# Gated attention and ternary feed-forward block: another order of the step on all engines, quantiser halves and evictions on ScalarE, scale factors on GpSimd

## What is computed

```python
x = x + tanh(g_xattn) * mlstm(layernorm(x), ctx, ctx)   # 8 heads of 64
x = x + tanh(g_ffn)   * ffn(layernorm(x))
# mlstm, a head: log_D[i,j] = cs[i] - cs[j] + ig[j], j <= i;  D = exp(log_D - rowmax)
#   C = (q @ k.T / 8) * D;  h = C / max(|sum C|, exp(-rowmax)) @ v;  then RMS norm of h
# ffn: g, u = actq(x) @ ternary(w_gate).T, actq(x) @ ternary(w_up).T
#   h = relu(g)**2 * u;  out = actq(h) @ ternary(w_down).T
# actq: round(x * 127 / rowmax|x|), rescaled afterwards
```

## Time and profile before

| | |
|---|---|
| median of three runs | 704.64 us |
| profiled execution, its own time | 707.75 us |
| span of the profile | 706.0 us |
| TensorE matmul busy | 602.2 us, 85% |
| VectorE busy | 568.5 us, 81% |
| ScalarE busy | 424.0 us, 60% |
| GpSimd busy | 97.9 us, 14% |
| mean granted TensorE clock | 0.944 of full |

### The profile page before, as it was taken

The page is one execution under the profiler, slowest core; times in us unless marked ns, Lnnn a source line. Parts: engine busy times, 40 slices in busy tenths (PEclk is TensorE's granted clock), DMA queues, the critical chain, the costliest instruction groups (busy, mean ns, idle before and its releaser), DMA issues.

```text
span 706.0 us, 18248 instructions
## 1 busy us (share of the span) xinstructions
PE 602.2 (85%) x6596; PEld 347.4 (49%) x6596; DVE 568.5 (81%) x1288; ACT 424.0 (60%) x893; POOL 97.9 (14%) x170
## 2 busy tenths in 40 slices
PE   7384776989989898998989898989989898989887
PEld 4151433545545454554646454555546464556443
DVE  4388559797879879697988979797979889797965
ACT  4376894657466465757556565657466565666542
POOL 1165020101001010101001010101000010101000
PEclk9797888999999999999999999999999999999999
DMA  9945201304040220404040230405040311402000
GB/s 311 381 160 177 85 0 56 127 17 165 3 165 15 97 82 15 164 0 164 15 164 15 64 116 15 164 0 179 0 164 15 108 72 38 144 17 76 2 30 31
DMA packets 45168, 63.73 MB, mean 90 GB/s; under 512 B 1872, under 2 KB 26704, under 8 KB 45136
## 3 DMA queue, kind: packets, MB, share of 16 engines
q1 hardware_dynamic: 43024, 61.19, 24.8%
q10 hardware_dynamic: 2112, 2.11, 0.9%
HBM read 54.77 MB, written 8.52 MB: 90 GB/s over the span
## 4 chain that ended last, share of the span: by engine, by line
DVE 31%; PE 29%; issue 20%; ACT 12%; DMA 5%; DVEq 1%; POOL 1%; SPq 0%; ACTq 0%; POOLq 0%
PE gb L1032 9%; PE ub L1032 7%; ACT dmat L528 4%; DVE stage L721 4%; PE yb L1055 4%; DVE dmat L824 3%; DVE hmaxes L729 3%; PE ab L1063 3%; DMA dmat<-max_rows 3%; ACT dmat L522 2%; PE tp L1076 2%; DVE ssq L842 2%; DVE amax L883 2%; PE ab L1043 2%; DVE x L865 1%
## 5 line engine op out<-in xcount | busy, mean ns | idle before, releaser
L1032 PE MATMUL gb<-wgT,xqT 128*128 128x512 bf16 x512 | 145.3, 410 | 4.9 <-ACT xqT L509 2.8
L1032 PE MATMUL ub<-wuT,xqT 128*128 128x512 bf16 x512 | 141.9, 403 | 0.9 <-DVE stage L721 0.9
L1055 PE MATMUL yb<-wdT,stage 128*128 128x512 bf16 x512 | 120.6, 379 | 2.0 <-ACT stage L502 1.9
L488 ACT ACTIVATE relu<-gb 128x512 f32<-128x512 f32 x128 | 75.6, 590 | 50.7 <-PE gb L1032 49.7
L721 DVE TENSOR_TENSOR stage<-relu,ub 128x512 f32<-128x512 f32 x128 | 86.7, 681 | 14.3 <-ACT relu L490 13.6
L424 POOL TENSOR_SCALAR_AFFINE_SELECT dmat<-dmat 128x256 f32<-128x256 f32 x128 | 50.1, 416 | 303.4 <-ACT dmat L528 303.4
L824 DVE SCALAR_TENSOR_TENSOR dmat<-ab,dmat 128x384 f32<-128x384 f32 x128 | 65.3, 551 | 26.3 <-POOL dmat L424 19.5
L1032 PEld LDWEIGHTS ub<-wuT,xqT 128*128 128x128 bf16 x512 | 52.4, 104 | 67.6 <-issue 17.2
L1063 PE MATMUL ab<-qT,cT 64*128 64x256 f32 x256 | 59.0, 436 | 29.5 <-DVE dmat L824 29.5
L490 ACT ACTIVATE relu<-relu 128x512 f32<-128x512 f32 x128 | 80.7, 630 | 4.0
L1055 PEld LDWEIGHTS yb<-wdT,stage 128*128 128x128 bf16 x512 | 48.7, 98 | 58.1 <-ACT stage L502 1.8
(11 more groups left out here) (108 smaller groups left out, 802.0 us busy)
## 6 DMA issues: line engine op xcount, KB each, us to landing
dmat<-max_rows SPq DMA_DIRECT2D x14, 1024.0 KB, 5.1
values<-in_ctx_v SPq DMA_DIRECT2D x16, 520.0 KB, 7.5
xs<-in_x SPq DMA_DIRECT2D x16, 512.0 KB, 5.8
cT<-in_ctx_t SPq DMA_DIRECT2D x16, 512.0 KB, 6.8
out<-stage SPq DMA_DIRECT2D x32, 256.0 KB, 2.1
stage<-in_w_gate SPq DMA_DIRECT2D x4, 1024.0 KB, 13.5
stage<-in_w_up SPq DMA_DIRECT2D x4, 1024.0 KB, 17.4
stage<-in_w_down SPq DMA_DIRECT2D x4, 1024.0 KB, 5.6
```

Of the source, the lines that this page charges most:

```text
L488: nc.scalar.activation(relu[:, c % 2, :], gb[c % 2][:, :], ACT.Relu).then_inc(g_free, 1)
L1032: last = nc.tensor.matmul(bank[c % 2][:, :], xqT[par][:, t, d, :], w[:, d, c * CH:(c + 1) * CH], start=(d == 0), stop=(d == KD - 1))
L1055: done = nc.tensor.matmul(yb[:, :], hqT[:, c, :], wdT[:, c, :], start=(c == 0), stop=(c == KF - 1))
```

## The change

It does five things.

1. The order of `step` on TensorE, ScalarE and VectorE is new. Scores, `weigh` and head outputs of n open the step, with the four chunks of the first tile between them. The front of m and the end of attention of n stand in the middle. The first pairs of heads of m are exponentiated and masked at the step's end, the other two pairs of n at its start. Second chunks, maxima and quantisation of the second tile come last.
2. The upper half of a hidden tile is quantised by ScalarE (`quantise_high`), the lower by VectorE (`quantise_low`). `hq` has two buffers.
3. Both halves of the transposed hidden tile leave PSUM through ScalarE.
4. `dd`, `dd2`, `c3` (`token_factor`) and `dq` (`hidden_factor`) are made by GpSimd; VectorE waits on `c3_ready` and `dq_ready`.
5. The maximum over a hidden row is folded by writing the first three chunks' maximum behind the row and reducing from there, in place of a separate maximum of two.

The diff, cut to its core, the indentation reduced. Of the four long `step` functions, all but GpSimd's and SyncE's are shown in their new order alone (lines added and kept); their old order is in the kernel above.

```diff
-GATE_K, POST_K, LN2_K = 3, 11, 16
-QUANT_K = 9
+GATE_K, POST_K, LN2_K = 3, 11, 13
+QUANT_K = 6
...
+HW = FF + 512
+h = [stage[1][:, HW * t:HW * t + FF + 1] for t in range(T)]
...
-hq = sb("hq", [P, FF], F16)
+hq = [sb(f"hq{t}", [P, FF], F16) for t in range(T)]
...
 def step(b, n, m, par):
+    if m is not None:
+        spread_max(m, par)
     if not at(b, 0):
         store(b - 1, 1)
-    store(b, 0)
-    if m is not None:
-        spread_max(m, par)
     if m is not None and not at(m, LAST):
         load(m + 1, 1 - par)
+    store(b, 0)
...
+def token_factor(n, npar):
+    gp.wait_ge(ln2_step, LN2_K * n + 10)
+    alone(gp, gp_passed)
+    nc.gpsimd.tensor_scalar(dd[:, :], am2[:, :], 1.0 / 127.0, 0.0, ALU.mult, ALU.add).then_inc(token_scale, 1)
+    gp.wait_ge(token_scale, 3 * n + 1)
+    nc.gpsimd.tensor_tensor(dd2[:, :], dd[:, :], dd[:, :], ALU.mult).then_inc(token_scale, 1)
+    gp.wait_ge(token_scale, 3 * n + 2)
+    if at(n, 0):
+        gp.wait_ge(winv_step, WINV[1] + 2)
+    alone(gp, gp_passed)
+    nc.gpsimd.tensor_scalar(dd2[:, :], dd2[:, :], wprod[:, 1:2], 0.0, ALU.mult, ALU.add).then_inc(token_scale, 1)
+    gp.wait_ge(token_scale, 3 * n + 3)
+    nc.gpsimd.tensor_tensor(c3[npar][:, :], dd2[:, :], dd[:, :], ALU.mult).then_inc(c3_ready, 1)
+def hidden_factor(b, t):
+    gp.wait_ge(quant_step, QUANT_K * (2 * b + t) + 3)
+    if at(b, 0) and t == 0:
+        gp.wait_ge(winv_step, WINV[2] + 1)
+    alone(gp, gp_passed)
+    nc.gpsimd.tensor_scalar(dq[:, t:t + 1], hm1[:, t:t + 1], wprod[:, 2:3], 0.0, ALU.mult, ALU.add).then_inc(dq_ready, 1)
...
+token_factor(0, 0)
+masks(1, 0)
+masks(1, 1)
 def step(b, n, m, par):
-    if n is None:
-        return
-    for p in range(NP):
-        masks(n, p)
+    if n is not None:
+        masks(n, 2)
+        masks(n, 3)
     if at(b, 0):
         scale_weight(2, 0)
         scale_weight(2, 1)
-    residual(n, 1 - par)
+    hidden_factor(b, 0)
+    if n is not None:
+        residual(n, 1 - par)
+        token_factor(n, 1 - par)
+    hidden_factor(b, 1)
+    if m is not None:
+        masks(m, 0)
+        masks(m, 1)
...
 def hidden_cols(b, t):
-    act.wait_ge(a_full[0], hidden_use(b, t) + 1)
     if not (at(b, 0) and t == 0):
         act.wait_ge(y_full, 2 * b + t)
-    nc.scalar.activation(hqT[:, 0:KF // 2, :], abh[0].rearrange("p (k s) -> p k s", s=P), ACT.Copy,
-                         bias=-MAGIC16).then_inc(a_free[0], 1)
+    for e in range(2):
+        act.wait_ge(a_full[e], hidden_use(b, t) + 1)
+        nc.scalar.activation(hqT[:, e * KF // 2:(e + 1) * KF // 2, :], abh[e].rearrange("p (k s) -> p k s", s=P), ACT.Copy,
+                             bias=-MAGIC16).then_inc(a_free[e], 1)
+def quantise_high(b, t):
+    act.wait_ge(quant_step, QUANT_K * (2 * b + t) + 5)
+    nc.scalar.activation(hq[t][:, FF // 2:], h[t][:, FF // 2:FF], ACT.Copy, scale=hqs[:, t:t + 1],
+                         bias=MAGIC16).then_inc(hq_high, 1)
...
+exponentials(1, 0, 1)
+exponentials(1, 1, 1)
 def step(b, n, m, par):
     npar = 1 - par
     prev = not at(b, 0)
     third = at(b, 0)
+    if n is not None:
+        exponentials(n, 2, npar)
+        exponentials(n, 3, npar)
     relu_square(b, 0, 0)
+    if n is not None:
+        heads(n, 0)
     if third:
         magnitudes(2, 0, 4)
+    relu_square(b, 0, 1)
+    if m is not None:
+        attention_rstd(m)
+    if n is not None:
+        heads(n, 1)
+    if third:
+        magnitudes(2, 1, 5)
+    relu_square(b, 0, 2)
+    if n is not None:
+        heads(n, 2)
+        heads(n, 3)
+    if m is not None:
+        for t in range(T):
+            columns(m, qT[par], t)
+    relu_square(b, 0, 3)
+    if n is not None:
+        squares(n)
     if prev:
         hidden_cols(b - 1, 1)
     if third:
         magnitudes(2, 2, 6)
         magnitudes(2, 3, 7)
+    if m is not None:
+        forget_gate(m)
+    if n is not None:
+        head_rms(n)
+    quantise_high(b, 0)
     relu_square(b, 1, 0)
     if third:
         scale_weight(2, 2)
         scale_weight(2, 3)
         sign_weight(2, 0, 4)
+    relu_square(b, 1, 1)
+    if n is not None:
+        tokens_rstd(n)
+    hidden_cols(b, 0)
+    if third:
         sign_weight(2, 1, 4)
+    relu_square(b, 1, 2)
+    if n is not None:
+        quantise_second(n)
+    if m is not None:
+        exp_minus_max(m, par)
     if third:
         sign_weight(2, 2, 4)
         sign_weight(2, 3, 4)
     relu_square(b, 1, 3)
+    if m is not None:
+        exponentials(m, 0, par)
+    quantise_high(b, 1)
     if n is not None:
         tokens(n, npar)
+    if m is not None:
+        exponentials(m, 1, par)
...
 def hidden_max(b, t, part):
-    split = (3, 2)[t]
-    first, last = ((0, split), (split, NC))[part]
-    dve.wait_ge(h_done, 8 * b + 4 * t + last)
-    nc.vector.tensor_reduce(hmaxes[:, t, part:part + 1], h[t][:, first * CH:last * CH], axis=AX_X, op=ALU.max,
-                            apply_absolute_value=True).then_inc(quant_step, 1)
-
-def quantise_hidden(b, t, par):
-    hidden_max(b, t, 1)
+    if part == 0:
+        dve.wait_ge(h_done, 8 * b + 4 * t + 3)
+        nc.vector.tensor_reduce(h[t][:, FF:FF + 1], h[t][:, 0:3 * CH], axis=AX_X, op=ALU.max,
+                                apply_absolute_value=True).then_inc(quant_step, 1)
+    else:
+        dve.wait_ge(h_done, 8 * b + 4 * t + 4)
+        dve.wait_ge(quant_step, QUANT_K * (2 * b + t) + 1)
+        nc.vector.tensor_reduce(hmax[:, t:t + 1], h[t][:, 3 * CH:FF + 1], axis=AX_X, op=ALU.max,
+                                apply_absolute_value=True).then_inc(quant_step, 1)
+def hidden_scale(b, t, par):
     k = QUANT_K * (2 * b + t) + 2
+    if t == 0:
+        dve.wait_ge(c3_ready, b + 1)
     dve.wait_ge(quant_step, k)
-    nc.vector.tensor_tensor(hmax[:, t:t + 1], hmaxes[:, t, 0:1], hmaxes[:, t, 1:2], ALU.max).then_inc(quant_step, 1)
-    dve.wait_ge(quant_step, k + 1)
+    if not (at(b, 0) and t == 0):
+        dve.wait_ge(dq_ready, 2 * b + t)
     nc.vector.tensor_scalar(hm1[:, t:t + 1], hmax[:, t:t + 1], c3[par][:, t:t + 1], QUANT_EPS,
                             ALU.mult, ALU.max).then_inc(quant_step, 1)
+    dve.wait_ge(quant_step, k + 1)
+    nc.vector.reciprocal(rhm[:, t:t + 1], hm1[:, t:t + 1]).then_inc(quant_step, 1)
     dve.wait_ge(quant_step, k + 2)
-    nc.vector.reciprocal(rhm[:, t:t + 1], hm1[:, t:t + 1]).then_inc(quant_step, 1)
-    dve.wait_ge(quant_step, k + 3)
     nc.vector.tensor_scalar(hqs[:, t:t + 1], rhm[:, t:t + 1], c3[par][:, t:t + 1], 127.0,
                             ALU.mult, ALU.mult).then_inc(quant_step, 1)
-    dve.wait_ge(quant_step, k + 4)
-    if at(b, 0) and t == 0:
-        dve.wait_ge(winv_step, WINV[2] + 1)
-    for e in range(2):
-        half = slice(e * FF // 2, (e + 1) * FF // 2)
-        nc.vector.tensor_scalar(hq[:, half], h[t][:, half], hqs[:, t:t + 1], MAGIC16, ALU.mult, ALU.add).then_inc(quant_step, 1)
-    nc.vector.tensor_scalar(dq[:, t:t + 1], hm1[:, t:t + 1], wprod[:, 2:3], None, ALU.mult).then_inc(quant_step, 1)
-
-def hidden_cols(b, t):
-
-    dve.wait_ge(a_full[1], hidden_use(b, t) + 1)
-    if not (at(b, 0) and t == 0):
-        dve.wait_ge(y_full, 2 * b + t)
-    nc.vector.tensor_scalar(hqT[:, KF // 2:KF, :], abh[1].rearrange("p (k s) -> p k s", s=P), MAGIC16, None,
-                            ALU.subtract).then_inc(a_free[1], 1)
+def quantise_low(b, t):
+    dve.wait_ge(quant_step, QUANT_K * (2 * b + t) + 5)
+    nc.vector.tensor_scalar(hq[t][:, 0:FF // 2], h[t][:, 0:FF // 2], hqs[:, t:t + 1], MAGIC16,
+                            ALU.mult, ALU.add).then_inc(quant_step, 1)
 def output(b, t, xpar):
     k = 2 * b + t
     dve.wait_ge(y_full, k + 1)
-    dve.wait_ge(quant_step, QUANT_K * (k + 1))
+    dve.wait_ge(dq_ready, k + 1)
...
-        dve.wait_ge(o_ready, 2 * n - 2)
+        dve.wait_ge(o_ready, 2 * n - 3)
...
-    nc.vector.tensor_scalar(dd[:, :], am2[:, :], 1.0 / 127.0, None, ALU.mult).then_inc(ln2_step, 1)
-    dve.wait_ge(ln2_step, k + 14)
-    nc.vector.tensor_tensor(dd2[:, :], dd[:, :], dd[:, :], ALU.mult).then_inc(ln2_step, 1)
-    dve.wait_ge(ln2_step, k + 15)
-    nc.vector.scalar_tensor_tensor(c3[npar][:, :], dd2[:, :], wprod[:, 1:2], dd[:, :], ALU.mult, ALU.mult).then_inc(ln2_step, 1)
-    dve.wait_ge(ln2_step, k + 16)
...
 def step(b, n, m, par):
     npar = 1 - par
     prev = not at(b, 0)
     if n is not None:
         weigh(n, 0)
         weigh(n, 1)
+    hidden(b, 0, 0)
     if n is not None:
         weigh(n, 2)
         weigh(n, 3)
     if m is not None:
+        attention_stats(m, par)
+    hidden(b, 0, 1)
     if n is not None:
         weigh(n, 4)
         weigh(n, 5)
+    if m is not None:
+        attention_norm(m, par)
     if n is not None:
         weigh(n, 6)
         weigh(n, 7)
+    hidden(b, 0, 2)
+    hidden_max(b, 0, 0)
+    if n is not None:
+        normaliser(n, npar)
+    hidden(b, 0, 3)
+    if n is not None:
+        head_squares(n)
+    if m is not None:
+        gates_in(m)
+    hidden_max(b, 0, 1)
+    if m is not None:
```

(55 more changed lines are left out.)

142 lines of the change are left out of this document (30 added, 112 removed).

## The result

The changed kernel takes 741.79 us (median of four runs, 741.18 to 742.85) beside 704.27 us for the kernel before on the same chip: a ratio of 1.052, with a 95% interval of 1.0491 to 1.0549. The forecast was 731 us, in a range of 706 to 755. It is slower, as forecast, by 37.5 us where 26 were expected. The profiled execution of after has a time of 742.85 us.

The account below looks back on a forecast made before the run. VectorE's queue was taken to carry the step. A walked chain of 41.1 us plus 0.2 clock and 0.3 port gave 41.6, +1.86 times 13 = +24.2; with ends +1.8, +26: 733.8 profiled, median 731 us, range 706 to 755.

Parts of the forecast that it names:

- (a): Step's start on ScalarE: rest of `tokens` copy, three exponential pairs, relu and square before VectorE's `hidden(b,0,0)`; 5.8 us.
- (b): VectorE next: `hidden`, two `weigh`, stats of m, `hidden`, `weigh` 4 and 5; 4.8 us, ending at 10.6.
- (c): TensorE from scores 7: scores, chunk 2, heads 2, `q_columns`, heads 3; 5.3 us, ending at 15.9.
- (f): VectorE's run of 8.18 us in its new places, plus quantiser half, scan, maximum and others; 13.4 us, ending at 36.0.
- (g): New ScalarE wait: last chunk's relu stands behind `exp_minus_max(m)`, which needs `negated_max(m)`; 1.45 us, ending at 37.5.
- (i): Step's end on ScalarE: quantiser half, 1.05 us, ahead of `tokens`, 0.59; ending at 41.1.
- the clock: TensorE slow after its pause, on first scores and chunk, off the chain; delays relu of chunk 1 by 0.2 us.
- the ends: Steps outside the steady stretch: step 0 +3.3 us, step 14 +0.8, last step -2.3; together +1.8.
- GpSimd's port: VectorE held up beside new small GpSimd operations; bounds 0 and 1.0 us, taken as 0.3 a step.
- The faster case: Rival, chance 0.12: ScalarE's exponentials fit into its quantiser wait, relu and square over before 1.8 us; step 37.6, 678 us.
- The two cancel: Rival, chance 0.08: `negated_max` comes in time and port waits are nil; 39.8 to 40.0 us a step, 707 us.
- The clock as the whole cause: Rival, chance 0.15: TensorE stays at 1.2 GHz into (c); 759 us if every second step, 787 if every step.

Follow-up runs that it names:

- g1: Kernel before, in its old order, with only the four scale factors (dd, dd2, c3, dq) moved to GpSimd; 685.51 us, ratio 0.9742.
- e1: Changed kernel with `relu_square(b,1,3)` ahead of `exp_minus_max(m)` on ScalarE, nothing else; 723.35 us, ratio 1.027.
- u1: Changed kernel with both upper quantiser halves back on VectorE; 706.83 us, ratio 1.002.
- e5: Changed kernel with 16 products on constants filling TensorE's pause before the scores; 739.37 us, ratio 1.0503.
- f2: Changed kernel with the three ScalarE reorderings of e4 and both quantiser halves back on VectorE; 680.12 us, ratio 0.9635.
- p2: Kernel before, in its old order, with only the upper quantiser halves and both hidden-tile evictions on ScalarE; 741.05 us, ratio 1.0527.
- p3: Kernel before, in its old order, with only both hidden-tile evictions on ScalarE; 728.11 us, ratio 1.0336.
- e6: Changed kernel with the edits of e2 and e5 together; 735.87 us, ratio 1.0448.
- e2: Changed kernel with `relu_square(b,0,0)` ahead of the exponentials of heads 4 to 7 on ScalarE; 753.94 us, ratio 1.0698.
- u2: Changed kernel with both quantiser halves and the upper eviction back on VectorE; 720.77 us, ratio 1.022.
- e4: Changed kernel, ScalarE reordered: last relu ahead of `exp_minus_max`, `tokens` ahead of an exponential pair and quantiser half, first relu ahead of exponentials; 702.34 us, ratio 0.9962.

## Why the prediction was right, and where it was off

**The view that it started from.** That VectorE's queue carries the step of before held for the steps at full speed: g1 takes 0.76 us out of its unbroken run and they shorten by 0.6. It left out that before loses more to the slow clock than after does, 1.5 us a step (39.74 on average, 38.22 at full speed) against 0.6. Between the shortest steps the change costs 3.2 us, between the means 2.2. That the relief of VectorE in this change goes into idle time held too: 30.7 us busy, 11.3 idle in a step, against 10 forecast.

**The walk.** Taken from the end of the first `tokens` copy (416.94 + 0.59 = 417.53), the marks of one step of after, measured against forecast:

| step | mark | forecast | measured |
|---|---|---|---|
| (a) | `hidden(b,0,0)` starts, 423.32 | 5.8 | 5.79 |
| (b) | `weigh` 5 over, 427.53 + 1.01 | 10.6 | 11.0 |
| (c) | heads 3 over, 433.15 + 0.92 | 15.9 | 16.5 |
| (d) | relu and square of chunk 3 over, 436.69 | 18.5 | 19.2 |
| (e) | scale of the first tile over, 440.77 | 22.6 | 23.2 |
| (f) | `negated_max` over, 454.13 | 36.0 | 36.6 |
| (g) | `hidden(b,1,3)` starts, 455.56 | 37.5 | 38.0 |
| (h) | second scale over, 457.80 | 39.45 | 40.3 |
| (i) | first `tokens` copy over, 459.44 | 41.1 | 41.9 |

Each row was worked out from durations of the kernel before, and no mark is off by more than 0.9 us. Part of the lag from (b) on is the slow first chunk of this step. In (a) small errors cancel: the rest of the copy took 0.47 for 0.4, the exponentials 4.04 for 4.15. Two marks were then tried: (g) alone by e1 (1.4 us a step for 1.45), and the half and wait at (i), together with the first tile's half, by u1. Step (a), three pairs of exponentials ahead of the first relu, stays at 5.8 us when TensorE's clock is mended (e5).

**What failed is the size of two terms.** The first is the clock, 0.2 us a step. The steps of after have three lengths, near 41.4, 41.9 and 42.6, with a mean of 41.96. The shortest is the forecast without the clock term (41.1 + 0.3 = 41.4), so the clock costs 0.6 a step, 7.3 us in all where 2.6 were counted. e5, with most of the pauses filled, bears this out: eleven of its 13 steps take 41.1 to 41.7. The step that failed is "that falls on the first scores and chunk, off the chain". Here is the chain that ended last (start us, us, what) in a short step:

```profile
500.24 1.06 ACT xqT L550 x2
...
504.94 0.50 ACT dmat L569
505.44 0.49 ACT relu L522
505.95 0.64 ACT relu L524
...
507.22 1.01 DVE dmat L870 x2
...
510.90 0.81 PE ab L1123 x3
```

and in a long one:

```profile
374.32 0.59 ACT xqT L550
...
377.08 1.82 PE gb L1089 x4
378.91 1.71 PE ub L1089 x4
380.61 1.09 PE ab L1123 x4
...
386.32 0.77 PE ab L1123 x3
```

The short step goes as walked: exponentials, relu, VectorE, and at 10.1 us after the copy's end (500.83) TensorE's scores. In the long one the first chunk takes 3.53 us instead of 2.2 (503.34 to 505.54), and the second scores, heads and the next chunk stand behind it in TensorE's queue; the chain never leaves TensorE up to heads 3. Two branches lead into (c), and the slow clock makes the other one the later. Wherever the second half of that chunk takes 1.6 to 1.9 us for its four products, the step is 41.9 to 42.7; where it takes 1.03 to 1.17, 41.2 to 41.4.

The second is the ends. Step 0 was put at +3.3 and is +4.75; its `hidden(0,0)` of 118.65 waits 5.21 us for a relu. The last two steps were put at +0.8 and -2.3 and came to +2.4 and -0.8. Together +6.3, where +1.8 was counted. I had summed them from single operations instead of walking their queues as the steady step was walked. Between the two profiled executions the forecast had 26 us and the runs 35.1: 4.6 of the 9.1 missing lie in the steady steps and 4.5 in the ends. The rest of the 10.8 us is that the profiled execution of before stands 3.1 above its median and that of after 1.1.

**GpSimd's port** was taken at 0.3 us a step. It is seen where it was expected, at the end of the step: `quantise_low` takes 0.89 us beside the masks of m and 0.75 alone (440.77), and two masks take 1.22 beside it and 0.77 alone. The Trainium skill's page "SBUF — State Buffer", section "Who interferes with whom", has the later of the two fully blocked for the other's instruction. The trace agrees that they disturb each other; by that rule VectorE could have lost the 0.4 us of a mask, and it lost 0.14. `dq` and the factors took 0.19 to 0.27 us and held VectorE up nowhere on the path. That the shortest step meets 41.4 is therefore partly luck: 0.3 us of port that is hardly there against 0.3 of small terms that are.

**The rivals.** The faster case (0.12) named its deciding point and its size: relu and square before VectorE asks for them, 37.6 us a step, 678 us. The written order excludes it in the changed kernel, where relu and square end at 5.8. f2 comes to 37.5 us a step and 680.12, but that is not the rival come true: it also drops the wait of (g) and gives the halves back, and VectorE still waits 0.85 us before `hidden(b,0,0)`. That the numbers meet is chance. "The two cancel" was excluded by `negated_max` coming just as late as walked. The clock as the whole cause was excluded by e5. Two sums of the rivals are off by a little and touch neither the forecast nor the range: a step of 40.4 us gives 715 us, not 713, and steps of 39.8 to 40.0 give 2.6 to 5.2 us more than before, not 2 to 4.

**What the walk did not tell** is what each part of the change is worth. By its steps the halves should cost one operation of 1.05 at (i); u1 shows 2.3 a step, 1.9 between the shortest steps, because the operation brings a wait for another engine's result into a queue in which `tokens`, the exponentials and the next relu stand behind it. That wait is in the walk's total, but my expectation for u1 (7 us of gain, 35 measured) priced the operation alone. A walk gives the length of a schedule; the worth of a part comes only from a second walk without it.

What stays open: why the ends cost what they do was not tried apart, and no run has the folded maximum alone. No run of the old order holds TensorE's clock fixed, so the parts of p2, p3 and g1 are split by the kinds of their steps and not by an experiment. What TensorE stands still for in five steps of e5 and e6 is not known.

## What to carry to other kernels

Before work is moved to an engine with idle time, look at what stands behind it in that engine's queue and whether the work waits for a third engine there: ScalarE was idle 15 us of 40, and the two halves there, the second with a wait of 0.9 us in front of it, cost 2.3 us a step. Take from the bound engine what lies inside its unbroken run and give it to a queue on which nobody waits (four small operations on GpSimd: 2.6%, in part by fewer slow chunks); a larger relief outside that run or into a busy queue can cost 5%. When steps come in two lengths, compare long with long and short with short before a difference is laid to the work that was moved. And when a wait is to be removed by reordering, walk one engine further: e2 alone lost 12 us, and the same edit was part of the best version once its input came earlier.

## What the runs showed of the hardware

The slow clock falls after the pause, not only in it, and differs from step to step under the same pause. In the changed kernel TensorE is idle 4.14 to 4.20 us before the scores of twelve of the 13 steady steps, and the eight products of the first chunk take 1.49 + 1.6, 1.89 + 1.91, 1.89 + 1.13 or 1.33 + 1.03 us (the first half sometimes three of its four). After 2.13 us idle in u1 the scores run at full speed (0.96 for three of them, 1.28 in after) and the chunk behind them at half. In the kernel before, 2.25 us idle is followed by 1.89 for four products and, one step later, 2.38 by 1.04. The Trainium skill's page "TensorE: Matmul & The Clock Gate", section "What's actually happening", has two levels and a default to the lower one; the two durations of a chunk, near 1.9 and 1.03, agree.

The length of the pause alone does not decide. In u1 and u2 TensorE is idle 2.09 to 2.14 us before the scores of the same twelve steps; nine of them have a slow chunk in u1 and two in u2. Nor does a slow chunk always cost: of u1's nine such steps one is longer (40.84 us), the others take 39.4 to 39.6. Here are the 13 steady steps of the profiled executions, from the first `tokens` copy of a step to that of the next. A slow chunk is one with four products in over 1.12 us, where full speed is 1.03.

| kernel | mean step, us | steps with all chunks at full speed: number, mean | steps with a slow chunk: number, mean |
|---|---|---|---|
| before | 39.74 | 4, 38.22 | 9, 40.41 |
| g1 | 38.00 | 10, 37.64 | 3, 39.23 |
| p3 | 41.00 | 0 | 13, 41.00 |
| p2 | 41.75 | 0 | 13, 41.75 |
| after | 41.96 | 0 | 13, 41.96 |
| e5 | 41.62 | 11, 41.39 | 2, 42.88 |
| u1 | 39.64 | 4, 39.66 | 9, 39.64 |
| e4 | 39.33 | 6, 38.55 | 7, 40.00 |
| f2 | 37.62 | 13, 37.62 | 0 |

A higher granted clock is no gain by itself: e5 raised it from 0.916 to 0.958 for 2.4 us. In f2 it is 1.00 in the steady stretch, with the pause before the scores down to 0.46 us.

The upper half of a quantised row on ScalarE (1024 columns from SBUF to float16, with a scale for each partition) took 1.15 us, 1.06 from start to start; the bounds had been 1.02 and 1.44.
